# Graph attention, linear attention and a mixture of experts in one kernel: one-hot matrices in float32, logit parts summed in PSUM, messages shared evenly by two engines

## What is computed

```
feat = (xn @ W).reshape(N, 4, 64);  el = sum(feat * attn_l);  er = sum(feat * attn_r)
e     = leaky_relu(el[src] + er[dst], 0.2)            # one number per edge and head
alpha = exp(e - emax[dst]) / segment_sum(exp(e - emax[dst]), dst)
rst   = segment_sum(feat[src] * alpha, dst) + bias
gnn   = xn + elu(rst)
mix   = linear attention of xn (8 heads, feature map elu + 1, kv and k summed over all nodes)
x     = x + gnn + mix
x     = x + moe(layernorm(x))                         # router, top 2 of 8 experts, 256 -> 1024 -> 256
```

## Time and profile before

| | |
|---|---|
| median of three runs | 1895.49 us |
| profiled execution, first to last instruction | 1890.1 us |
| PE / PEld / DVE / ACT / POOL busy | 1581.7 / 1300.0 / 1368.5 / 1079.1 / 1218.3 us |
| TensorE clock granted, mean | 0.937 of full speed |

### The profile page before, as it was taken

The page is one execution under the profiler, slowest core; times in us unless marked ns, Lnnn a source line. Parts: engine busy times, 40 slices in busy tenths (PEclk is TensorE's granted clock), DMA queues, the critical chain, the costliest instruction groups (busy, mean ns, idle before and its releaser), DMA issues. The chain is left out here.

```text
span 1890.1 us, 46784 instructions
## 1 busy us (share of the span) xinstructions
PE 1581.7 (84%) x11358; PEld 1300.0 (69%) x11358; DVE 1368.5 (72%) x3833; ACT 1079.1 (57%) x3043; POOL 1218.3 (64%) x1135
## 2 busy tenths in 40 slices
PE   7858777788787989888887778629999999999995
PEld 5635555455566777777775666517888889888884
DVE  6656567677667888888888999897666656665662
ACT  4655566566666666677666776563444444444441
POOL 2077777777777777777677776105666666666663
PEclk8978899999999999999998888658999999999998
DMA  7745565566544555555555665652333333333332
GB/s 223 247 122 138 168 174 164 165 176 179 150 117 127 155 150 150 141 152 145 142 139 179 183 202 162 200 199 45 53 48 53 49 48 50 53 50 49 46 53 24
DMA packets 149158, 239.37 MB, mean 127 GB/s; under 512 B 27536, under 2 KB 114824, under 8 KB 147624
## 3 DMA queue, kind: packets, MB, share of 16 engines
q0 software_dynamic: 61216, 132.39, 30.4%
q1 hardware_dynamic: 85944, 103.15, 16.8%
q10 hardware_dynamic: 1744, 0.85, 0.2%
HBM read 180.78 MB, written 55.52 MB: 125 GB/s over the span
## 5 line engine op out<-in xcount | busy, mean ns | idle before, releaser
L843 POOL DMA_INDIRECT w_s<-table,w_s x784 | 806.4, 1029 | 279.9 <-issue 231.4
L2092 PE MATMUL bank<-w_s 128*128 128x260 f32 x1952 | 515.9, 410 | 110.3 <-DVE w_s L1536 110.0
L2092 PEld LDWEIGHTS bank<-w_s 128*128 128x128 f32 x1952 | 378.1, 201 | 206.0 <-DVE w_s L1536 139.9
L1026 ACT ACTIVATE w_s<-w_s 128x64 f32 x976 | 260.3, 337 | 68.3 <-ACT w_s L1021 68.1
L1536 DVE SCALAR_TENSOR_TENSOR w_s<-w_s 128x256 f32<-128x256 f32 x732 | 275.7, 426 | 26.7 <-ACT w_s L1026 18.9
L2294 PE MATMUL bank<-acc,w_s 128*128 128x256 f16 (+1 forms) x2736 | 290.4, 265 | 1.6 <-DVE acc L1937 1.5
L2315 PE MATMUL bank<-w_s,acc 128*128 x2520 | 284.5, 273 | 7.2 <-DVE acc L1951 5.5
L907 POOL DMA_INDIRECT out<-mid_g,low_g x105 | 177.2, 1687 | 151.2 <-ACT mid_g L1197 90.6
L2294 PEld LDWEIGHTS bank<-acc,w_s 128*128 x2736 | 252.9, 98 | 30.7 <-issue 2.1
L2315 PEld LDWEIGHTS bank<-w_s,acc 128*128 128x128 f16 x2520 | 245.8, 98 | 37.0 <-issue 8.7
L1033 ACT COPY w_s<-bank 128x512 bf16<-128x512 bf16 x244 | 142.1, 582 | 202.8 <-PE bank L2072 202.3
(11 more groups left out here) (308 smaller groups left out, 2187.6 us busy)
## 6 DMA issues: line engine op xcount, KB each, us to landing
stage<-in_L_ffn_W SPq DMA_DIRECT2D x32, 512.0 KB, 4.2
w_s<-table,w_s POOLq DMA_INDIRECT x784
w_s<-in_x SPq DMA_DIRECT2D x48, 256.0 KB, 4.0
w_s<-xT_d SPq DMA_DIRECT2D x96, 128.0 KB
w_park<-low_g SPq DMA_DIRECT2D x18, 512.0 KB
w_s<-w_park SPq DMA_DIRECT2D x9, 1024.0 KB, 9.1
xn_d<-acc SPq DMA_DIRECT2D x7, 896.0 KB, 5.0
table<-w_s SPq DMA_DIRECT2D x24, 260.0 KB, 3.5
```

Source lines behind the costliest of these rows:

```text
L843: pool.indirect_dma_start(out=ring[:, u, k, :], out_offset=None, in_=table[:, :], in_offset=bass.IndirectOffsetOnAxis(ap=srcT[:, (q * RING ...
L1026: last = act.activation(m[:, e, 0:GD], rows[:, e, 0:GD], ACT.Copy, scale=m[:, e, GD:HC])
L2092: last = pe.matmul(bank[2 + k.at % 2][:, 0:ROW], hot32[:, k.at % 4, s, :], msg[:, k.at % 2, s, :], start=s == 0, stop=s == SUB - 1)
```

## The change

- The one-hots are made in float32 at once, in a ring `hot` of six (HOTS). `hot16`, `hot32`, the cast on ScalarE and its semaphore go. TensorE transposes the float32 matrices.
- The three parts of the target product are added in PSUM by an accumulating matmul each: 12 matmuls of 8 columns, not 4 of 24. VectorE's part 0 goes, and its first and last remaining parts read PSUM. Since the last one reads it too, the next target product waits for the whole logit of the step before.
- ScalarE multiplies two sub-blocks of messages (OWN = 2; eight instructions), VectorE two; the second of these waits for ScalarE's part.
- The order within a slot of VectorE and TensorE is another. VectorE keeps walk words in three registers, and GpSimd masks its wait value with 255.

```diff
+HOTS = 6
+OWN = 2
...
-        turned16 = bank[0][:, 0:256].bitcast(BF16).rearrange("p (s c) -> p s c", s=SUB)
-        at_target = bank[1][:, 0:SUB * 3 * 2 * GH].rearrange("p (s c) -> p s c", s=SUB)
+        turned_hot = bank[0][:, :].rearrange("p (s c) -> p s c", s=SUB)
+        at_target = bank[1][:, 0:SUB * 2 * GH].rearrange("p (s c) -> p s c", s=SUB)
...
-                        pool.wait_ge(msg_ready, pool.snap(free_r[u], min_val=1, max_val=J))
+                        pool.wait_ge(msg_ready, pool.snap(pool.snap(free_r[u], min_val=1, max_val=J) & 255).with_bounds(min_val=1, max_val=J))
...
             def act_slot(j):
                 if (j + 3).live():
                     act_hotT(j + 3)
-                if (j + 2).live():
-                    act_hot32(j + 2)
...
-                act.wait_ge(logit_turn, 4 * k.n + 4)
+                act.wait_ge(logit_turn, 3 * k.n + 3)
...
-                for e in range((SUB - 1) * GH, SUB * GH):
+                for e in range((SUB - OWN) * GH, SUB * GH):
...
             def dve_slot(j):
...
-                if scores:
-                    dve_logit(j + 1, None, None, 0)
-                if (j + 3).live():
-                    dve_hot(j + 3, ...)
                 if scores:
...
-                    dve_logit(j + 1, group1, slot1, 1)
+                    dve_logit(j + 1, group1, slot1, 0)
                 if (j - 2).live():
                     dve_add(j - 2, ...)
                 if scores:
+                    dve_logit(j + 1, group1, slot1, 1)
+                if j.live():
+                    dve_msg(j, own_slot, 0)
+                if scores:
                     dve_logit(j + 1, group1, slot1, 2)
+                if (j + 3).live():
+                    dve_hot(j + 3, ...)
                 if j.live():
-                    dve_msg(j, ...)
-                if scores:
-                    dve_logit(j + 1, group1, slot1, 3)
+                    dve_msg(j, own_slot, 1)
...
-                if k.past(4):
-                    dve.wait_ge(hot_turned, k.n - 3)
-                    dve.wait_ge(hot32_ready, k.n - 3)
-                dve.scalar_tensor_tensor(hot16[:, k.at % 4, :, :],
+                if k.past(HOTS):
+                    dve.wait_ge(sum_ready, k.n - HOTS + 1)
+                dve.scalar_tensor_tensor(hot[:, k.n % HOTS, :, :],
...
-                if n == 0:
-                    last = dve.tensor_reduce(goal[:, k.at % 2, :, :], at_target.rearrange("p s (c k) -> p s k c", c=3), AX.X, ALU.add)
...
             def pe_slot(j):
+                if (j + 2).live():
+                    pe_target(j + 2)
                 if (j + 3).live():
                     pe_turn(j + 3)
-                if (j + 2).live():
-                    pe_target(j + 2)
...
-                    last = pe.transpose(turned16[:, s, :], hot16[:, k.at % 4, s, :], ident16[:, :])
+                    last = pe.transpose(turned_hot[:, s, :], hot[:, k.n % HOTS, s, :], ident[:, :])
...
-                    pe.wait_ge(logit_turn, 4 * k.n - 3)
+                    pe.wait_ge(logit_turn, 3 * k.n)
                 for s in range(SUB):
-                    last = pe.matmul(at_target[:, s, :], hotT[:, k.at % 2, s, :],
-                                     target3[:, bass.ds(tile, 1), :, :].rearrange("p a b c -> p (a b c)"), start=True, stop=True)
+                    for c in range(3):
+                        last = pe.matmul(at_target[:, s, :], hotT[:, k.at % 2, s, :],
+                                         target3[:, bass.ds(tile, 1), c, :].rearrange("p a b -> p (a b)"), start=c == 0, stop=c == 2)
...
-                pe.wait_ge(hot32_ready, k.n + 1)
```

More of the change, by code:

```diff
@@ L281, in build @@
         msg = walk([P, 2, SUB, ROW])
-        hot16 = walk([P, STEPS, SUB, P], BF16)
-        hot32 = walk([P, STEPS, SUB, P])
+        hot = walk([P, HOTS, SUB, P])
         hotT = walk([P, 2, SUB, P], BF16)
@@ L304, in build @@
         far_i = walk([1, 1], I32)
-        hot_f = hot32[:, 0, :, :]
-        off_f = hot32[:, 1, :, :]
-        far_v = hot32[:, 2, :, :]
+        hot_f = hot[:, 0, :, :]
+        off_f = hot[:, 1, :, :]
+        far_v = hot[:, 2, :, :]
         far_rows = msg[:, 0, :, :]
@@ L1463, in _, with load_step @@
                     lambda: dve.tensor_scalar(inverse, inverse, 1.0, None, ALU.add))
[L1470 to L1473 removed]
+            walk_r = [dve.alloc_register(f"walk{u}") for u in range(3)]
+            def load_step(n):
+                dve.load([walk_r[n % 3]], walk_i[0:1, bass.ds(n + 3, 1)])
             def dve_slot(j):
[L1476 to L1477 removed]
+                word = dve.snap(walk_r[j.n % 3], min_val=0, max_val=WORDS - 1)
+                last = dve.snap(walk_r[(j.n - 1) % 3], min_val=0, max_val=WORDS - 1)
                 scores = (j + 1).live()
[L1479 to L1482 removed]
                 if scores:
@@ L1527, in dve_logit, with dve_msg @@
                 last.then_inc(logit_turn, 1)
-            def dve_msg(k, slot):
-                dve.wait_ge(weight_ready, k.n + 1)
+            def dve_msg(k, slot, part):
+                if part == 0:
+                    dve.wait_ge(weight_ready, k.n + 1)
+                else:
+                    dve.wait_ge(part_ready, k.n + 1)
                 m, rows = heads_at(msg[:, k.at % 2, :, :]), ring_heads(slot)
-                for e in range(0, (SUB - 1) * GH, GH):
-                    if e == (SUB - 2) * GH:
-                        dve.wait_ge(part_ready, k.n + 1)
+                for e in range(part * (SUB - OWN - 1) * GH, (SUB - OWN - 1 + part) * GH, GH):
                     last = dve.scalar_tensor_tensor(m[:, e:e + GH, 0:GD], rows[:, e:e + GH, 0:GD], 1.0,
                                                     m[:, e:e + GH, GD:HC].to_broadcast([P, GH, GD]), ALU.mult, ALU.mult)
-                last.then_inc(msg_ready, 1)
+                if part:
+                    last.then_inc(msg_ready, 1)
             def dve_add(k, tile):
@@ L2091, in pe_sum @@
                 for s in range(SUB):
-                    last = pe.matmul(bank[2 + k.at % 2][:, 0:ROW], hot32[:, k.at % 4, s, :], msg[:, k.at % 2, s, :],
+                    last = pe.matmul(bank[2 + k.at % 2][:, 0:ROW], hot[:, k.n % HOTS, s, :], msg[:, k.at % 2, s, :],
                                      start=s == 0, stop=s == SUB - 1)
```

35 lines of the change are left out of this document (13 added, 22 removed).

## The result

The changed kernel takes 1959.87 us (median of four runs, 1957.24 to 1961.42) against 1895.84 for the kernel before on the same chip: a ratio of 1.034, 95% interval 1.0315 to 1.0358. The profiled execution spans 1959.7 us against 1890.1. The forecast was 1936 us with a range that ends at 1960, 0.1 us above the median; two of the four runs are outside it.

The account below looks back on a forecast made before the run. Gathers bound the first stage, a chain through several engines the second, VectorE the third. Terms -1 + 38 + 4 = +41 us take 1890.1 to 1931 us, 1936 with 5.4 us to the median; 8-in-10 range 1888 to 1960.

Parts of the forecast that it names:

- the second stage: Queries beside the walk, 392.3 us, 24 turns, bound by a chain through several engines: forecast +38 us (+28 to +46).
- (a): ScalarE, second stage: cast goes, four products come, 0.45 us more a slot, two slots in the chain: +0.90 us a turn.
- (b): Slot 3 on TensorE, second stage: slower float32 transposes and eight more target matmuls: +0.35 us a turn.
- (c): Slot 0 on TensorE, second stage: target product now ahead of the transposes, which are slower: +0.55 us a turn.
- The turn: Second stage, transposes of slot 0 to those of the next turn: 16.43 us growing to 18.2 us.
- (d): VectorE: gains 0.46 us a step, off the chain; moved one-hot makes a second loop, 2.8 us, hidden under ScalarE's 2.92.
- (e): TensorE's target product newly waits for the whole logit of the step before: costs 0, up to 0.7 us without cover.
- First stage: Keys beside the walk, 492.0 us, paced by gathers; 137.8 us of waits cover slower engines: -1 us (-20 to +10).
- Third stage: End of the walk, 194.4 us, VectorE-limited: its gain against a loop lengthened by lumps, +4 us between -19 and +20.
- VectorE as the limit: Rival: the chain gives way if ScalarE's slot 1 ends no later; stages two and three faster, 1860 us; chance 0.12.
- Nothing much changes: Rival: the order in the slot frees as much as the added work takes, 1895 to 1900 us; chance 0.10.
- All three stages slow: Rival: the walk's own loop also passes the gathers' pace in the first stage, +30 there, 1966 us; chance 0.08.

Follow-up runs that it names:

- before_hot32: The kernel before with one-hots made in float32 in a ring of six and no cast on ScalarE: 1891.3 us, ratio 0.9973 to 1.0000.
- hot32_own2: before_hot32 with two sub-blocks of messages on ScalarE: 1930.1 us, ratio 1.0152 to 1.0202.
- after_old_order: The changed kernel with the one-hot ahead of the first message and logit part, transposes ahead of the target product: 1949.9 us.
- after_own1: The changed kernel with one sub-block of messages on ScalarE and three on VectorE: 1953.9 us, ratio 1.0288 to 1.0343.
- after_own1_copy_old_order: after_own1_copy with the order undone, one-hot ahead of the message and transposes ahead of the target product: 1900.8 us.
- before_psum: The kernel before with only the three logit parts summed in PSUM, its order kept: 1946.6 us, ratio 1.0251 to 1.0322.
- before_own2: The kernel before with only the messages moved, two sub-blocks each on ScalarE and VectorE: 1971.3 us, ratio 1.0355 to 1.0471.
- after_copy: The changed kernel with VectorE copying the sums out of PSUM at the head of its slot: 1983.7 us, ratio 1.0437 to 1.0473.
- after_own1_copy: The changed kernel with one sub-block on ScalarE and VectorE copying the sums out of PSUM first: 1986.6 us, ratio 1.0457 to 1.0505.

## Why the prediction came out as it did

The sign, the stage and the chain were right. The size was 24 us short of the median and 29 us of the profiled span (+69.6 against +41): the second stage was 9.5 us short, the third 10.3, the first 4.9, and 3.9 lie outside the three. That the median is inside the range, by 0.1 us, is luck.

The sum also adds 5.4 us between span and median. The changed kernel's profiled execution took 1961.42 us over a span of 1959.7, so the two lie 1.7 us apart, and it was itself the slowest of its four; most of the 5.4 was that the kernel before was profiled in an execution faster than its median. Of the span's miss this hides some 5 us in the median.

The runs give a path from the kernel before to the changed one, one part at a time: float32 one-hots without the cast, -4 us (before_hot32); two sub-blocks on ScalarE, +38 (hot32_own2); sums in PSUM with the wait for the whole logit, +20 (after_old_order); the new order, +10. A part's price depends on what is already there: two sub-blocks cost 75 us with the cast kept and 38 without it, and taking them out of the changed kernel gives back 6.

**(a) ScalarE's slots**, forecast +0.90 a turn, measured 0.56 + 0.44 = 1.00. The products cost what was forecast (2.02 against 1.06 us for a slot). The cast gave back less in slot 0, since from the copy's start to the exponent's are 0.61 us, where 0.48 was left by the sum. It isn't the copy from float32, which was costed at 0: its median is 585 ns, as from bfloat16, and in slot 1 the exponent does start 0.48 us behind it. Why the exponent starts later in slot 0 is not shown.

**(b), (c) TensorE's slots 3 and 0**, forecast +0.35 and +0.55, measured +0.40 and +0.56.

**The turn** was forecast at 18.2 and is 18.32. Times 24 that is 45 us. The step that failed in the second stage is the deduction behind it, from 43 to 38 us, for waits for gathers that a slower walk absorbs and for the shorter last turns: the stage grew by 47.5 and gave nothing back, though the waits for gathers did fall, from 6.1 us to 0.4.

**(d)** The second loop was costed at some 2.8 us a step. The changed kernel's timeline has them at 3.36, from one-hot to one-hot:

```profile
861.91 0.74 DVE L1493 SCALAR_TENSOR_TENSOR w_s<-w_s,iota 128x512 f32<-128x512 f32 x1
...
862.76 0.63 PE L2061 MATMUL bank<-ident,w_s 128*128 128x128 f32 x4
...
863.43 0.58 ACT L1024 CAST w_s<-bank 128x512 bf16<-128x512 f32 x1 [0.39 <-PE bank L2061]
...
864.05 0.23 ACT L1012 ACTIVATE w_s<-w_s 128x16 f32<-128x16 f32 x1
...
864.79 0.42 DVE L1524 SCALAR_TENSOR_TENSOR w_s<-w_s 128x256 f32<-128x256 f32 x1
...
865.12 0.23 DVE L1513 SCALAR_TENSOR_TENSOR w_s<-bank,w_s 128x16 f32<-128x16 f32 x1
865.27 0.74 DVE L1493 SCALAR_TENSOR_TENSOR w_s<-w_s,iota 128x512 f32<-128x512 f32 x1
```

The terms were given without hand-overs, for which the sum had some 0.2 us in all. From start to start, one-hot to transposes is 0.85 us (0.74 in the sum), transposes to copy 0.67 (0.6), copy to exponent 0.62 (0.5), exponent to message 0.74 (0.25), where VectorE is still at the addition and at the logit's second part. The prediction's own condition, that this loop is shorter than ScalarE's slot, did not come true: 3.36 against 3.03. In the second stage of the changed kernel "hidden" did hold all the same, since its turn, with the work for the queries in it, is still the first chain. But after_own1 shows how little lies behind: with four products a slot gone, and one message of 0.33 us a step more on VectorE, its turn is 17.92 us. after_own1_copy_old_order shows that the one-hot's place behind the exponent is what holds it in the kernel with the copy; for after_own1 itself this is inferred.

**(e)** was costed at 0, up to 0.7 us. For the second stage of the changed kernel that stands: TensorE waits 2.2 us there for the last part of the logit. Outside of it the wait is there, 38.1 us in the first stage and 39.7 in the third, but a wait is not yet a cost: after_old_order has 46.1 us of it in the first stage, which is 7 us shorter. Where it did cost, 38 us, is before_psum, in the order of before.

**First stage**, -1 forecast, +3.9 measured, within its bounds. The cover of 137.8 us shrank to 78.2. VectorE's smaller work did not shorten the gathers: GpSimd is busy 378.38 us for 374 of them, 376.95 before. The median of one is unchanged:

```profile
L842 POOL DMA_INDIRECT w_s<-table,w_s x784: 940/946/2637, 97.4 to 1247.2; - x196
```

By the rule cited ahead (SBUF — State Buffer, the Trainium skill, on contention) VectorE's two-input instructions don't hold up the descriptors, and nothing was to be had; the trace agrees in this stage. The masked wait value isn't seen either: GpSimd's "issue" time ahead of the gathers is 108.5 us here against 111.7. No run has the mask alone.

**Third stage**, +4 forecast from bounds of -19 and +20, +14.3 measured. The mechanism was named, and the prediction's own loop gave the size: 4.75 us a step, which over 44 steps is 15 us more than before; measured are 208.7 / 44 = 4.74, so near in part by chance, since the last stretch has no lumps. What failed is the place taken between the bounds, +4, for which VectorE's gain was weighed against that loop; VectorE is busy 158.5 of the 208.7 us now, 76%, where it was 91%. after_old_order gives a price: 9 of the 14 us are the order. That a lump on VectorE now delays the one-hot and the last logit part together is how I read it; no run moves the lumps.

**Not foreseen**: the load of the next step's word on VectorE, 40.8 and 30.9 us of "issue" in the two long stages, about 0.42 us each. Before, it stood behind the messages, and "issue" ahead of the addition is 1.0 us in the second stage. In the changed kernel it is part of the 0.74 us between exponent and message above; nothing here shows a price for it.

**The rivals.** VectorE as the limit fell with its own condition: ScalarE's slot 1 ends later. "Nothing much changes" fell with (b) and (c), which came in full. The changed kernel's clock did not fall (0.938 of full speed against 0.937; 1.00 in the second stage). "All three stages slow" was nearest in size, at 1966 us, but its mechanism isn't there: the changed kernel's first stage grew by 3.9 us and not by 30. A longer first stage did show in before_own2 (by 26 us) and in the two kernels with one sub-block and the new order (by 15 and 21).

**Open**: why after_old_order's turn is 0.8 us over that of hot32_own2. The twelve products are some 0.2 of it in slot 3; in its slot 0 ScalarE's exponent starts 1.16 us after the copy and not 0.62, and the releaser that the trace names, the first logit part of the next step, is by the code not what it waits for. And why the copy in after_copy costs 24 us: the trace shows 44.7 us of waiting in 86 steps of the second stage between the copy and the first part, with the word load in it, and the one-hot later by that much would explain the waits of the transposes; but no run takes that load away.

## What to carry to other kernels

A chain read link by link from one turn forecasts the turn well (18.2 against 18.3), but a saving on it is worth only the distance to the next loop, so cost the second loop as carefully as the first, hand-overs included: here undoing the part that cost most on the path gave back a tenth of the loss. Dropping a small reduction that copies out of PSUM can be dear: it was what freed the bank for the next product. And an instruction that starts another engine's work, as the one-hot does, belongs ahead of those that wait, not behind them: that was worth 10 us in the changed kernel and 86 in after_own1_copy.

## What the runs showed of the hardware

Matmuls with eight columns of output cost little each: twelve accumulating ones take 0.45 us, four with 24 columns 0.25. A one-hot of 128x512 takes 744 ns on VectorE, the median, whether it writes bfloat16 or float32. Four transposes of float32 take 0.64 us against 0.39 for bfloat16, and the copy of 128x512 out of PSUM 585 ns, the median, from either type. A register load on VectorE behind a short instruction leaves it idle for about 0.42 us; behind the messages nearly nothing of it was seen.
